# Moving every large on-chip tensor of a transformer-block kernel to multiples of 256 bytes

## The reference, cut to what matters

```python
x = x + _layernorm(_L0_attn_ref(_layernorm(x), ...))
x = x + _layernorm(_L0_ffn_ref(_layernorm(x), ...))

# attention-like stage, on n = LN(x)
W1 = gelu(n @ h1_w1 + h1_b1) @ h1_w2 + h1_b2
W2 = gelu(n @ h2_w1 + h2_b1) @ h2_w2 + h2_b2
W3 = tril(W1 @ W2.T)
t  = LN(gelu(W3 @ n));  x1 = x + t
out = x + gelu(LN(x1) @ fm_w1 + fm_b1) @ fm_w2 + fm_b2

# feed-forward stage, ternary weights with a scale for each output
h = silu(x @ w1.T * s1) * (x @ w2.T * s2)
h = gelu(h @ hw1.T * hs1);  h = gelu(h @ hw2.T * hs2)
y = h @ w3.T * s3
```

## The kernel before, in words

| tensors | before | after |
|---|---|---|
| `X`, `attn_w_hi`, `attn_w_lo`, `ffn_w_hi`, `ffn_w_lo`, `raw`, `cols` | 128 | 0 |
| `bc` | 32 | 160 |
| `ident`, `mask` | 160 | 32 |
| `NF`, `XR`, `XRB`, `n_tok`, `M`, `TG`, `OTA`, `aT`, `mT`, `yT`, `h1T`, `h2T`, `sc`, `h_hidden`, `fm_hidden`, `ffn_gate`, `ffn_h1` (high and low parts) | 160 | 0 |
| the small tensors of the normalisations, 8 to 96 bytes each | any multiple of 32 | 96 more |

## Time and profile before

### The profile page before, as it was taken

One profiled execution on the slowest core, in us unless ns is written; L12 is line 12 of the kernel. 1 busy time (PEld: TensorE's weight loads), 2 busy tenths in 40 slices (PEclk: granted clock), 3 DMA queues, 4 the chain that ended last, 5 costly groups with the idle time before them and its releaser, 6 DMA issues.

```text
span 363.5 us, 6043 instructions
## 1 busy us (share of the span) xinstructions
PE 351.9 (97%) x1786; PEld 290.1 (80%) x1786; DVE 319.9 (88%) x953; ACT 302.2 (83%) x546; POOL 153.2 (42%) x227
## 2 busy tenths in 40 slices
PE   6999999999999999999999999999999999999991
PEld 5886888788888888888888888888788878778990
DVE  5989999999999999899968999998878998958844
ACT  5999999996888979976789798889698489769890
POOL 3587868430581165109430276025450292053311
PEclk9999999999999999999999999999999999999998
DMA  7614300000000000000000000001010001000101
GB/s 231 174 58 148 114 4 1 0 3 0 3 0 0 2 9 23 0 0 2 1 29 3 0 2 2 0 0 32 1 31 0 0 2 31 0 2 0 32 30 32
DMA packets 8946, 9.08 MB, mean 25 GB/s; under 512 B 720, under 2 KB 6864, under 8 KB 8912
## 3 DMA queue, kind: packets, MB, share of 16 engines
q1 hardware_dynamic: 8368, 8.41, 7.7%
q10 hardware_dynamic: 544, 0.26, 0.3%
HBM read 6.57 MB, written 2.10 MB: 24 GB/s over the span
## 4 chain that ended last, share of the span: by engine, by line
PE 78%; ACT 10%; DVE 6%; issue 2%; DMA 1%; SPq 0%; POOLq 0%; POOL 0%; DVEq 0%; ACTq 0%
PE bank L1236 10%; PE bank L1234 10%; PE bank L1250 8%; PE bank L1251 8%; PE bank L1111 4%; PE bank L1115 4%; PE bank L1112 4%; PE bank L1130 4%; PE bank L1127 4%; PE bank L1128 4%; PE bank L1216 4%; PE bank L1219 4%; PE bank L1055 3%; ACT h_hidden_hi L511 3%; ACT bank L516 2%
## 5 line engine op out<-in xcount | busy, mean ns | idle before, releaser
L722 DVE TENSOR_TENSOR ffn_gate_lo<-bank,ffn_gate_hi 128x512 fp32r<-128x512 f32 (+1 forms) x72 | 43.9, 623 | 8.8 <-ACT bank L587 7.9
L511 ACT ACTIVATE h_hidden_hi<-bank,cols 128x512 fp32r<-128x512 f32 x64 | 43.7, 697 | 7.7 <-PE bank L1115 7.0
L587 ACT ACTIVATE bank<-bank,cols 128x512 f32<-128x512 f32 (+1 forms) x72 | 44.1, 640 | 0.7
L722 DVE TENSOR_TENSOR h_hidden_lo<-bank,h_hidden_hi 128x512 fp32r<-128x512 f32 x64 | 42.3, 677 | 0.4 <-ACT bank L516 0.2
L516 ACT ACTIVATE bank<-bank,cols 128x512 f32<-128x512 f32 x64 | 41.9, 670 | 0.3
L1234 PE MATMUL bank<-ffn_gate_hi,ffn_w_hi 128*128 128x512 f32 (+1 forms) x108 | 40.4, 379 | 0.0
L1236 PE MATMUL bank<-ffn_gate_lo,ffn_w_hi 128*128 128x512 f32 (+1 forms) x108 | 39.6, 373 | 0.0
L581 ACT ACTIVATE ffn_h_hi<-bank,cols 128x512 fp32r<-128x512 f32 (+1 forms) x36 | 23.2, 647 | 13.2 <-PE bank L1236 9.5
L369 POOL TENSOR_TENSOR XR<-X,ln_x_r 128x512 f32<-128x512 f32 x8 | 8.3, 1041 | 52.5 <-DVE bank L867 51.3
L581 ACT ACTIVATE ffn_gate_hi<-bank,cols 128x512 fp32r<-128x512 f32 (+1 forms) x36 | 23.7, 679 | 7.2 <-PE bank L1236 4.3
L1216 PE MATMUL bank<-yT_hi,ffn_w_hi 128*128 128x512 f32 (+1 forms) x72 | 27.0, 379 | 0.2 <-ACT raw L604 0.2
(11 more groups left out here) (162 smaller groups left out, 1118.9 us busy)
## 6 DMA issues: line engine op xcount, KB each, us to landing
raw<-ffn_w SPq DMA_DIRECT2D x5, 512.0 KB, 3.6
out<-X SPq DMA_DIRECT2D x7, 256.0 KB, 2.3
raw<-attn_w SPq DMA_DIRECT2D x6, 256.0 KB, 4.9
X<-x SPq DMA_DIRECT2D x3, 256.0 KB, 5.1
raw<-ffn_w SPq DMA_DIRECT2D x1, 256.0 KB, 3.1
X<-x SPq DMA_DIRECT2D x1, 128.0 KB, 2.4
X<-x ACTq DMA_DIRECT2D x1, 128.0 KB, 2.7
out<-X SPq DMA_DIRECT2D x1, 128.0 KB, 1.9
```

What stands on the lines that cost most here:

```text
L511: nc.scalar.activation(dst, bank(f"{L}u{j}", c)[:, :], ACT.Gelu, bias=bias_of(L, j)).then_inc(*hi[L].done(c, j))
L587: nc.scalar.activation(u, u, ACT.Gelu, scale=cols[:, C_HS[L] + j:C_HS[L] + j + 1]).then_inc(*act2[L].done(c, j))
L722: return nc.vector.tensor_tensor(dst, whole, high.bitcast(f32), ALU.subtract)
```

## The change

A tensor of 128 bytes a partition, `ahead`, is placed before all others and used by nobody. The two scratch columns become the two columns of one tensor, which takes one place of 32 bytes instead of two. Everything up to the scratch columns thereby moves up by 128 bytes, everything behind them by 96. The instructions of each engine, their order, their waits and their sizes are the same in both programs.

```diff
--- before.py
+++ after.py
@@ -116,6 +116,7 @@
         def halves(name, shape):
             return [sb(f"{name}_{h}", shape, f32r) for h in ("hi", "lo")]
 
+        sb("ahead", [P, 32])
         X = sb("X", [P, TILES, D])
         Aw, Fw = halves("attn_w", [P, 6 * DI]), halves("ffn_w", [P, ffn_w.shape[1]])
         raw = sb("raw", [P, 6 * DI])
@@ -129,7 +130,8 @@
         ones = sb("ones", [P, 1])
         lo_sums, lo_any = sb("lo_sums", [P, FP]), sb("lo_any", [P, FP])
         lo_flag = sb("lo_flag", [1, 1])
-        warm, quiet = sb("warm", [P, 1]), sb("quiet", [P, 1])
+        warm_quiet = sb("warm_quiet", [P, 2])
+        warm, quiet = warm_quiet[:, 0:1], warm_quiet[:, 1:2]
 
         NF, XR, XRB = sb("NF", [P, T, D]), sb("XR", [P, T, D]), sb("XRB", [P, T, D])
         n_tok = halves("n_tok", [P, T, D])
```

## The result

| | before | after |
|---|---|---|
| median | 364.96 us (364.9 to 365.11, 4 runs) | 360.74 us (359.82 to 361.63, 4 runs) |
| ratio | | 0.9884, 95% interval 0.9852 to 0.9915 |
| the profiled execution | 365.25 us, span 363.5 us | 360.05 us, span 358.3 us |

The change makes the kernel faster by 1.2%, by 4.2 us, with no instruction added, removed or moved. I had forecast no change, 364.95 us, in a range of 363.9 to 365.8 us.

A forecast was written before the change was run, and what follows sets the result against it. TensorE was taken to set the pace alone from 72 to 330 us. Every term was 0, so the sum was 0 against the profiled 365.25 us; the median, 364.95 us, was forecast, range 363.9 to 365.8 us.

The forecast's parts named there:

- What bounds the kernel, and which things a placement can change: TensorE alone sets the pace from 72 to 330 us; only matmul steps, other engines' durations, first loads or last stores can change.
- The stream of the matmuls, from 160 to 0: Large streamed matmul operands: taken as 0, bounded by 0.7 ns a matmul, 1.0 us over the 512- and 256-column matmuls.
- The pairs in the trace (128 against 160): Weight loads, VectorE, GpSimd and ScalarE take the same at both starts, within 2 ns, so they were taken as 0.
- The slower rival: Weight and stream reads on TensorE collide when in step: 8.2 us more, 373 us, chance 6%.
- the extrapolation from 256 to 512 columns: In the slower rival, 3.2 ns more at 256 columns was taken as 6.4 ns at 512, for 8.2 us in all.
- The faster rival: Matmul stream: the excess per column, 19.95 ns at 512 columns, belongs to the placement; 343 to 352 us, chance 7%.
- Weights, VectorE, ScalarE, GpSimd, transfers: 0: Weight loads, the other engines' instructions and the loads and stores were each forecast to change by 0.
- the lines of 256 bytes: Loads and last store: transfers off a 256-byte boundary touch one line more; gain bounded by 1.1 us, 363.85 us, chance 4%.
- The 0.38 us: Last store: by the skill's table 20 beats against 16, a fifth of 1.9 us saved, giving 364.6 us.
- What would show it: Signs: steps of 233.3 and 116.8 ns, durations within 2 ns, first transfer about 4.4 us, same TensorE share 72 to 330 us.
- the two stretches: Unbroken matmuls, 62 of 512 columns from 204.87 us and 256-column ones from 338.69 us; steps forecast unchanged, 233.3 and 116.8 ns.
- The range and the chances: Whole kernel: 363.9 to 365.8 us; no change 77%, faster by over 0.2% 14%, slower 9%.

The follow-up runs named there:

- the four profiled kernels at distance 0: Changed kernel twice (360.74, 361.21 us), only its scratch-column edit made to the kernel before (361.73 us), changed kernel with `ident` and mask at 0 (361.37 us).
- the six widths: TensorE alone, computation left out, matmuls of 128 to 512 columns at distances 0 and 32; 512 columns took 226.9 and 233.3 ns a step.
- the small kernel: TensorE alone, computation left out, 12 matmuls per pair of weight and stream starts; 512-column steps 226.7 to 228.0 ns at distance 0.
- distance 64: Kernel before with 32 bytes of padding behind the scratch columns, weights at 128, streams at 192: 362.14 us, ratio 0.9920.

## Why the prediction was wrong

**What bounds the kernel, and which things a placement can change.** Right. TensorE sets the pace from 72 us on, and the gain is made there: from the 361st matmul, at 75 us, to the last the four profiled kernels at distance 0 need 3.2 to 3.4 us less than before, while at the 361st itself they are between 0.3 us earlier and 0.3 us later. With the cheaper matmuls TensorE is a little less alone in this, as its new waits show.

**The stream of the matmuls, from 160 to 0, "the bounds are those above: paid once a matmul, at most 0.7 ns".** This is the step that failed. I had split the excess of two widths, 19.95 and 10.1 ns, into a part per matmul and a part per column, found nothing per matmul, and inferred that a start could cost nothing. The split needs an excess that is a line in the columns. It is none, as the six widths show, and 20 to 10 was an accident of distance 32 at these two widths. After the change the excesses are 13.7 and 13.3 ns, and the same split puts nearly all of it on the matmul. What the two placements differ by is 6.3 ns in 512 columns, where I had allowed 0.7.

**The pairs in the trace (128 against 160).** Each was read rightly and they stayed so after. But they compare one stream alone, or two streams on VectorE and GpSimd, and I carried them over to two reads on TensorE. The loads' equal 140 ns say how long a load takes, and not what the load does to the stream above it.

**The slower rival, "weights and stream start at the same rest".** It named the variable that decides, with the wrong sign for 512 columns: equal starts are the best case there. The rows on which it leaned, 120 ns against 116.8 in 256 columns, were not all rounding: over the whole trace of before such steps have a mean of 118.6 ns, and after the change, where the 256-column products near the end have equal starts too, those take 120.0. The rival fell with the extrapolation from 256 to 512 columns, where the sign turns.

**The faster rival, "by the matmuls".** The right place, with 7%. Its price was the whole excess, 347 us. The run takes back 6.3 of 20 ns, at 256 columns it gives 3.2 ns up, and not everywhere: behind a break of the 512-column stream the step starts high and falls. Mean steps by place in an unbroken sequence of 512-column matmuls, from the starts in the traces:

```
place            1-4    5-9    10-14  15-19  20-24
before, ns       232.0  233.4  233.1  233.5  233.3
after, ns        230.9  229.4  227.7  227.2  227.3
```

The means of all 512-column steps without a break are 233.0 before and 228.5 after, 4.5 ns apart and not 6.3. Over 1192 matmuls that would be 5.4 us; 3.4 us arrived. The step-by-step comparison above says where the rest is. The matmuls before the 361st, a fifth of them, gained nothing, since VectorE and ScalarE are full there, as I had said. Steps that end in a transpose or a break gained nothing either. The 256-column steps gave 0.4 us back, and waits at the breaks 0.3 us on balance.

**Weights, VectorE, ScalarE, GpSimd, transfers: 0.** Right by the rows, for the weights as far as the length of a load goes; as one end of the distance their start does count. The pad alone moves `X` and `raw` to 0 and gives 0.9992 (0.9979 to 1.0004), so the lines of 256 bytes are worth at most 0.8 us here, and most likely less. The 0.38 us that I had put beside the sum by the Trainium skill's "How a descriptor splits into AXI transactions" ("DMA: Bandwidth & Descriptors") lie within that interval: these runs neither show nor exclude them.

**What would show it.** One of the signs that I had named could not have told the cases apart. TensorE is busy for 257.58 of 258 us between 72 and 330 us, as before, but it starts 1275 matmuls there and not 1255: an engine that is always busy stays so when its work gets cheaper. Another held in part: durations stayed within 2 ns but for ScalarE's copy to `n_tok_hi`, 644 ns against 632. The steps of the two stretches were the sign that counted.

**The range and the chances.** The range was built on the bound that fell. The profile did hold a warning: a mean excess of 20 ns a matmul with no engine to blame for it, beside a placement (start 0, distance 0 for the large products) that the trace had never shown. That deserved more than 7%.

## What to carry to other kernels

Where TensorE is the bound and the matmuls are fp32r with 512 columns, look at the start-to-start time of an unbroken stretch (here with new 128 x 128 weights for every matmul): 233 ns had 6 ns to give, and no placement in these runs went below 227. Then print the byte addresses and compare where the weights and the streams begin, by 256; a pad between the two groups is enough, and equal starts matter, not round ones. Look at the other widths as well: with 256 columns equal starts cost up to 3 ns more. An excess seen at two widths is no evidence of how it is made up; a kernel of a few lines that runs all pairs tells more in 290 us than the argument did.

## What the runs showed of the hardware that I had not expected

- The cost of an fp32r matmul beneath which the next weights are loaded depends on the distance between the byte addresses of the stream and the weights, by 256: with 512 columns 226.7 ns at 0, 228.9 at 64, 232 to 235 at the other multiples of 32, 236.6 at 4. Over all 64 pairs of starts by 32 the starts themselves change this by 2 ns at most. Why the distance counts is open.
- At 256 columns the order is another (118.9 at 0, 117.9 at 32 in the small kernel; 120.0 and 116.8 in the full one), the distance does not decide alone (114 or 117.7 ns at 192), and at 448 equal starts cost 2.2 ns more than a distance of 32.
- The steps at distance 0, 119.7, 173.4, 206.7 and 226.7 ns, lie close to 18, 26, 31 and 34 times 6.67 ns, the time of 16 columns at 2.4 GHz. Others, as 117.7 and 204.5 ns at distance 32, do not. This is only read off, and no run tests what it means.
- In the full kernel the step falls behind a break from 231 to 227 ns in some 15 matmuls at distance 0, and from 231 to 229 at distance 64. At distance 32 it rises, from 232 to 233.
- bf16 is at 215.8 ns with 512 columns at all seven distances tried. This agrees with the 215.7 ns of the Trainium skill ("TensorE: Matmul & The Clock Gate", section "Wait — 56ns, not 53.3ns?"), which no fp32r stretch reached: the best was 11 ns above it.
